# A two-layer decoder on one core: feed-forward network in parts at both ends of its run, attention bank cleared by another engine

## The reference

```python
# layer 0
x = ln(x + attn(x))                       # one head of 128
x = ln(x + xattn(x, ctx_512))             # 16 heads of 8: over own tokens (causal) and over 1601 context tokens
x = ln(x + moe(x))                        # 8 experts, 2 of them per token
# layer 1
x = ln(x + recurrent(x))                  # complex linear recurrence over the tokens
x = ln(x + S((x Wq)(ctx Wk)^T) (ctx Wv))  # one head of 128, over the 1601 context tokens
g = silu(x W1 * s1) * (x W2 * s2)         # 128 -> 512, weights of -1, 0, 1 with a scale for each column
h = gelu(gelu(g H1 * sh1) H2 * sh2)       # 512 -> 512 -> 512
x = ln(x + h W3 * s3)                     # 512 -> 128
```

## Time and profile before

| | |
|---|---|
| median of 3 runs | 692.98 us (692.75 to 695.24) |
| profiled execution, its own time | 695.09 us |
| its span, first to last instruction | 692.1 us |
| PE busy | 610.8 us (88% of the span) |
| DVE busy | 526.6 us (76%) |
| ACT busy | 449.9 us (65%) |
| POOL busy | 205.5 us (30%) |
| mean granted clock of PE | 0.974 of 2.4 GHz |

### The profile page before, as it was taken

How to read it: one execution, slowest core, us unless ns; L and a number is a source line. 1 busy time by engine, 2 the same in 40 slices (tenths; PEclk the granted TensorE clock), 3 DMA queues, 4 the chain that set the end, 5 groups by cost and what they waited for, 6 DMA issues and landing times. The chain is left out here.

```text
span 692.1 us, 13555 instructions
## 1 busy us (share of the span) xinstructions
PE 610.8 (88%) x5182; PEld 332.9 (48%) x5183; DVE 526.6 (76%) x706; ACT 449.9 (65%) x813; POOL 205.5 (30%) x277
## 2 busy tenths in 40 slices
PE   8989899999999999999999874999819899888996
PEld 5645433333333333433333353788304566547883
DVE  5369889999999999999964463899589668767442
ACT  3556578888888888888887451556782256655324
POOL 7224532335455576676640030000000000014000
PEclk9999989999999999999999997999978999999999
DMA  8258575655666544333310069553000100000000
GB/s 206 98 152 278 167 214 182 145 121 140 163 165 159 141 112 98 92 82 89 91 37 2 6 227 408 162 159 111 1 0 0 43 4 0 2 1 0 1 0 30
DMA packets 43293, 70.74 MB, mean 102 GB/s; under 512 B 12492, under 2 KB 31652, under 8 KB 42720
## 3 DMA queue, kind: packets, MB, share of 16 engines
q1 hardware_dynamic: 31696, 38.34, 20.9%
q0 software_dynamic: 10928, 29.32, 13.1%
q10 hardware_dynamic: 608, 2.25, 1.4%
HBM read 44.41 MB, written 24.79 MB: 100 GB/s over the span
## 5 line engine op out<-in xcount | busy, mean ns | idle before, releaser
L962 ACT ACTIVATE prob<-ps 128x512 f32<-128x512 f32 (+2 forms) x480 | 253.1, 582 | 46.2 <-PE ps L738 39.1
L1083 DVE TENSOR_REDUCE pm<-ps 128x2 f32<-128x1024 f32 x192 | 226.0, 1216 | 6.6 <-PE ps L700 4.8
L761 PE MATMUL ps<-prob,vst 128*9 128x256 f32 (+1 forms) x1664 | 130.1, 385 | 10.1 <-ACT o_all L950 10.1
L738 PE MATMUL ps<-qq,kc 50*128 50x256 bf16 (+1 forms) x832 | 134.1, 275 | 0.1
L700 PE MATMUL ps<-kc,qq 48*128 48x512 bf16 x384 | 116.1, 387 | 3.2 <-DVE pm L1083 2.9
L738 PEld LDWEIGHTS ps<-qq,kc 50*128 50x128 bf16 (+1 forms) x832 | 52.2, 96 | 94.2 <-ACT prob L962 69.7
L761 PEld LDWEIGHTS ps<-prob,vst 128*9 128x9 f32 (+1 forms) x1664 | 25.1, 88 | 51.7 <-ACT prob L962 39.1
L1090 DVE TENSOR_REDUCE nm<-ps 128x4 f32<-128x512 f32 (+1 forms) x32 | 30.7, 958 | 14.9 <-PE ps L688 14.9
L1677 POOL DMA_DIRECT2D w_w<-in_w x2 | 1.1, 534 | 137.2 <-PE ps L1716 137.2
L700 PEld LDWEIGHTS ps<-kc,qq 48*128 48x128 bf16 x384 | 32.9, 93 | 13.3 <-DVE pm L1083 9.4
L688 PE MATMUL ps<-masks_b 64*128 64x256 bf16 x256 | 37.6, 269 | 0.0
(11 more groups left out here) (365 smaller groups left out, 1267.2 us busy)
## 6 DMA issues: line engine op xcount, KB each, us to landing
kc<-kc_scr SPq DMA_DIRECT2D x32, 300.2 KB, 4.9
comb_bc<-comb_scr SPq DMA_DIRECT2D x7, 512.0 KB, 4.8
below<-rden_scr POOLq DMA_DIRECT2D x13, 256.0 KB, 6.8
ctx<-ctx_scr POOLq DMA_DIRECT2D x1, 3204.0 KB, 17.0
raw<-in_wexp POOLq DMA_DIRECT2D x8, 384.0 KB, 3.5
exp_scr<-raw_high POOLq DMA_DIRECT2D x8, 384.0 KB, 3.9
exp_scr<-raw_low POOLq DMA_DIRECT2D x8, 384.0 KB, 4.9
kc_scr<-hi SPq DMA_DIRECT2D x6, 400.2 KB, 4.8
```

The lines of the kernel that those rows point to most:

```text
L738: last = pe.matmul(bank[0:p, j * TQ:(j + 1) * TQ], kc[s][rows, j, t * 128:t * 128 + p], qq[s][rows, 0, j, :], start=(j == 0), stop=True, s ...
L761: last = pe.matmul(o_ps[32 * hh:32 * hh + VW, kind * TQ + q0:(kind + 1) * TQ], value[:, hh * VW:(hh + 1) * VW], prob[0:k, (NST * n + t) % ...
L962: act.activation(prob[0:p, g % P_RING, 2 * e:2 * e + 2, q0:TQ], s2[0:p, k % S2_RING, 0:2 * w].rearrange("p (i q) -> p i q", i=2), ACT.Exp, ...
L1083: dve.tensor_reduce(pm[:, m % 2, c, :, jt], banks, AX.X, ALU.max).then_inc(s1_read, 1)
```

## The change

Three edits go together.

*Start of the first cross attention.* The DVE memset of `o_ps` is gone; ACT clears the bank by a copy of `X` times 0.0 behind its last copy of values. In steps 0 and 1, where there are no value products, PE issues two products of constants (128 x 512, bf16) each into the bank of the score ring that the next step overwrites. In step 1 it first waits for the two Exps of step 0.

*Front of the FFN.* ln5 of chunk 0 moves from the fourth group into the third (means at p = 4, variance at p = 5; the Ln and Exp follow at p = 0 of the fourth, DVE at p = 1), in other banks; the last weight parts move with it. DVE takes tile 0 (`gated(0)`) before the reciprocal of the fourth group. up(2) and up(3) get banks of their own and run without waiting for the attention's end; then 24 products of the first hidden layer (tiles 0 and 1) run feature by feature before up(4) to up(7). The first hidden layer gets four banks.

*End of the FFN.* The last layer of chunk 0 runs after six of the eight tiles of the second hidden layer, its residual and ln6 start among the last two tiles. Chunk 1 is taken in two parts of 256 columns from the last layer to the store.

```diff
-                    def keep_clock(count):
+                    def keep_clock(count, bank=0):
...
                         if g >= 2:
                             outputs((g - 2) // NST, (g - 2) % NST)
+                        else:
+                            if g:
+                                pe.wait_ge(exp_done, 2 * g)
+                            keep_clock(2, 2 * (g + 1) % S2_RING)
...
+                        if h == max(late_values):
+                            act.wait_ge(v_sb, DVE_VALUES)
+                            act.wait_ge(v_act, len(values_order) - DVE_VALUES)
+                            act.activation(o_ps, X[:, 0:CH], ACT.Copy, scale=0.0).then_inc(o_zero, 1)
...
-                            if m * HALVES + i == max(late_values) + 1:
-                                dve.wait_ge(v_act, len(values_order) - DVE_VALUES)
-                                dve.memset(o_ps, 0.0).then_inc(o_zero, 1)
...
-        HIGH_AT = {(1, 0): (0,), (1, 2): (1,), (1, 4): (2,), (2, 0): (3,), (2, 2): (4,), (3, 0): (5,), (3, 1): (6,)}
-        LOW_AT = {(1, 1): (0,), (1, 3): (1,), (1, 5): (2,), (2, 1): (3,), (2, 3): (4,), (3, 1): (5,), (3, 2): (6,)}
+        HIGH_AT = {(1, 0): (0,), (1, 2): (1,), (1, 4): (2,), (2, 0): (3,), (2, 2): (4,), (2, 4): (5,), (3, 2): (6,)}
+        LOW_AT = {(1, 1): (0,), (1, 3): (1,), (1, 5): (2,), (2, 1): (3,), (2, 3): (4,), (2, 5): (5,), (3, 3): (6,)}
...
-        UP, H1, H2, Y = ((0, 2), (4, 5), (6, 7)), (1, 3), (6, 7), (0, 2)
+        UP = ((0, 2), (4, 5), (1, 3), (0, 2), (1, 3), (6, 7), (0, 2), (1, 3))
+        UP_FREED = (None, None, None, 1, 3, None, 4, 5)
+        H1, H2 = (4, 5, 0, 2), (6, 7)
+        ends = [slice(0, CH), slice(CH, CH + CH // 2), slice(CH + CH // 2, 2 * CH)]
...
-                        if b == NB - 1 and p == 0:
+                        if b == NB - 2 and p == 4:
                             pe.wait_ge(s1_red, 2 * NB)
                             pe_ln5(0)
-                        if b == NB - 1 and p == 2:
+                        if b == NB - 2 and p == PAIRS - 2:
                             pe_ln5_v(0)
...
+                up(1)
+                up(2)
+                pe_ln5(1)
+                up(3)
+                pe_ln5_v(1)
+                pe.wait_ge(full_done, 2)
+                for i in range(NM):
+                    pe.wait_ge(ha_done, i + 1)
+                    for k in range(2):
+                        done = hidden_part("h1w", ha, H1[k], k, i)
+                        if i == NM - 1:
+                            done.then_inc(h1_ps, 1)
+                for k in range(NM, len(tiles)):
                     up(k)
-                    if k == 1:
-                        pe_ln5(1)
-                    if k == 2:
-                        pe_ln5_v(1)
...
+                for k in range(2, len(tiles)):
+                    first_hidden(k)
                 pe.wait_ge(split, split_by["h2w"])
-                hidden("h2w", hb, hb_done, H2, g2_done, h2_ps)
...
+                for k in range(6):
+                    second_hidden(k)
+                last_layer(0)
+                second_hidden(6)
                 pe_ln(0)
+                second_hidden(7)
+                pe_ln2(0)
+                last_layer(1)
+                last_layer(2)
                 pe_ln(1)
-                pe_ln2(0)
+                pe_ln(2)
                 pe_ln2(1)
+                pe_ln2(2)
```

More of the change, by code:

```diff
@@ L1660, in emit_rest @@
         pe_ln, pe_ln2, act_ln, _, dve_ln, x_ready, act_log, act_exp = ln_parts(
-            st, "ln6", ps[:, 4:6, :], ps[:, 6:8, :], r7_ready, apart=True, buffers=ln_buffers)
+            st, "ln6", LN6_C, LN6_V, r7_ready, apart=True, buffers=ln_buffers, spans=ends)
         tiles = [(c, m) for c in range(NCH) for m in range(NM)]
@@ L1667, in _ @@
             def _(sp):
-                for c in range(NCH):
+                for c, end in enumerate(ends):
                     sp.wait_ge(x_ready, c + 1)
-                    sp.dma_start(out[:, c * CH:(c + 1) * CH], X[:, c * CH:(c + 1) * CH]).then_inc(stored, 16)
-                sp.wait_ge(stored, 16 * NCH)
+                    sp.dma_start(out[:, end], X[:, end]).then_inc(stored, 16)
+                sp.wait_ge(stored, 16 * len(ends))
             @block.gpsimd
@@ L1890, in _, with hidden_part @@
-                hidden("h1w", ha, ha_done, H1, g1_done, h1_ps)
-                pe.wait_ge(split, split_by["h2w"])
-                hidden("h2w", hb, hb_done, H2, g2_done, h2_ps)
-                for c in range(NCH):
-                    pe.wait_ge(hc_done, NM * (c + 1))
-                    for i in range(NM):
-                        done = passes(ps[:, Y[c], :], (high_w["w3"][:, i, :], low_w["w3"][:, i, :]), 0,
-                                      [part[:, i, :] for part in hc[c]], i == 0, i == NM - 1)
-                    done.then_inc(y_ps, 1)
+                def hidden_part(name, src, bank, k, i):
+                    c, m = tiles[k]
+                    return passes(ps[:, bank, :], (high_w[name][:, i, :], low_w[name][:, i, :]), m,
+                                  [part[:, i, :] for part in src[c]], i == 0, i == NM - 1)
@@ new lines, in last_layer @@
+                def last_layer(n):
+                    end = ends[n]
+                    c = end.start // CH
+                    at = slice(end.start - c * CH, end.stop - c * CH)
+                    for i in range(NM):
+                        pe.wait_ge(hc_done, NM * c + i + 1)
+                        done = passes(Y[n], (high_w["w3"][:, i, :], low_w["w3"][:, i, :]), 0,
+                                      [part[:, i, at] for part in hc[c]], i == 0, i == NM - 1)
+                    done.then_inc(y_ps, 1)
```

120 lines of the change are left out of this document (72 added, 48 removed).

## The result

| | before | after |
|---|---|---|
| median | 694.11 us of 4 runs (692.75 to 695.89) | **684.24 us** of 4 runs (683.23 to 685.16) |
| profiled execution, its own time | 695.09 us | 683.23 us |
| its span | 692.1 us | 681.4 us |
| PE, DVE, ACT, POOL busy | 610.8, 526.6, 449.9, 205.5 us | 607.7, 526.3, 450.6, 205.7 us |
| mean granted clock of PE | 0.974 | 0.979 |

The ratio is 0.9856, 95% interval 0.9823 to 0.9889: 1.4% faster, and clear of no change. Forecast were 685.3 us and a range of 682.5 to 688.7. The engines do nearly the same work in both; what went are mostly waits and half-clock time of PE.

What follows compares the result with a forecast made beforehand. PE, busy 88% of the span, was taken as the bound, so shortening its list or gaps shortens the kernel. The terms -2.4 - 2.7 - 3.85 + 1.26 = -7.7 us took 692.98 to 685.3 us, range 682.5 to 688.7.

Steps and rivals of the forecast that it cites:

- A: Start of the first cross attention: 0.50 us of memset and 1.92 us of clock go, 2.4 us gained.
- Rival 1: Start of the first cross attention gains only the memset, 0.5 us; time 687.2 us; chance 0.17.
- B: Second cross attention, ln5 of chunk 0 a group earlier: fourth group 3.87 us shorter, third 1.17 late, 2.7 us gained.
- Rival 2: Second cross attention: the fourth group doesn't get shorter, as ACT waits for the sums; time 688.0 us; chance 0.08.
- C: Front of the FFN: PE's gaps and slow products shrink or go, a new wait of 0.26 us comes; 3.85 us gained.
- D: End of the FFN: chunk 1 as 24 narrow products for 12 wide ones costs 1.26 us.
- 0.1675 each: End of the FFN: price in us of a 256-column product with its weight load, 4.02 us for 24.
- Moving chunk 0 forward takes nothing off its list: End of the FFN: PE is gapless through the last layer, and chunk 0's products, means and variances stay.
- Nothing: End of the FFN: halving shortens last Ln and multiply by about 0.25 us each, extra hand-overs add about 0.4 together.
- narrow products at 0.115 us: End of the FFN: a sign that the prediction is wrong, if 256-column products pass at this time.
- rival 3: End of the FFN costs nothing, 24 narrow products taking 2.76 us; time 684.0 us; chance 0.08.
- Rival 4: Front of the FFN: waits for POOL's low parts drop the clock; 72 slow products give 698.7 us; chance 0.05.

Runs made afterwards that it cites:

- e2: The kernel before with the clear of the output bank moved from DVE to ACT, without constant products: 693.05 us, ratio 0.9983.
- e3: The kernel before with the four constant products added on PE and the memset left on DVE: 693.71 us, ratio 0.9979.
- e4: The kernel before with only ln5 of chunk 0 moved a group earlier: 692.47 us, ratio 0.996.
- e13: The changed kernel with one table set for the last norm and gated tile 0 put back behind the fourth group's residual: 684.05 us, ratio 0.9845.
- e12: The changed kernel with the end of the FFN as before the change, chunk 1 in one part: 685.41 us, ratio 0.9884.
- e6: The changed kernel with chunk 1 as one part of 512 columns at the end: 687.92 us, ratio 0.9919.
- e9: The changed kernel with the variance product of chunk 0 moved out of PE's stream, behind the last mean product but one: 687.39 us, ratio 0.9901.

## Why the prediction was right

The time was 684.24 us for 685.3 forecast, 1.1 us less. By steps, against the profile of before:

- **A, forecast 2.4, measured 2.96.** The mechanism holds in both halves (e2, e3). The memset is 0.61, not 0.50, and the clock the rest, as long as the constants are there; the shares shift with the order (e2). Its size depends on the course of the clock that the profile happened to show: against e4 it is 2.43, which the forecast met. My way of pricing it, by DVE's pace of a later unit at full clock, compared like with like and came within 0.6 of the 2.96. Rival 1 (only the memset) is out.
- **B, forecast 2.7, measured 2.81** (e4 alone 2.82). The fourth group is 3.82 us shorter for 3.87, the third pays 1.01 for 1.17. Rival 2 is out: ACT never waited for the sums.
- **C, forecast 3.85, measured 4.10.** The mean product came 6.34 us after up(0), as reckoned (618.64 - 612.30). The gap before it fell by 0.83 us, not 0.46, since up(2) ends later than my 12 x 0.230: the first product of up(1) has a bare load (0.42 us to the next), and the last one's row ends 0.40 us after its start, and only from there does the trace count the gap. The 1.98 us went, the slow products went (1.6 for 1.67), the new wait is 0.32 for 0.26. What I hadn't seen is that 1.6 us of this are not there in every execution, and that the tile put forward (gated 0) costs 0.35 us at the end instead of helping (e13).
- **D, forecast +1.26, measured +0.67, by other steps than mine.** This is the term that failed. "0.1675 each" was read from four products in the chain of waits; there the first weight load of the four starts only when the products before it are through, and is bare (0.19 us), so the four are 0.19 + 4 x 0.12. The load's row is below; the split is argued from it, not tested. In the stream narrow products follow each other at 0.119: 24 take 2.86 us, +0.10. Here the formula of the Trainium skill that the prediction set against the row (109 ns) was nearer than the row. "Moving chunk 0 forward takes nothing off its list" was wrong as well, since it adds: two norm products inside the stream, 0.86 us each (0.46 of their own, 0.40 of loads behind them that nothing covers), and 0.20 us at the last tile, whose cover (the last layer of chunk 0) had been moved ahead of it. That is 1.92 us, beside the 1.77 that e12 and e6 leave for the order. By e9 the second of the two norm products costs nothing by itself, since PE would wait there anyway. "Nothing" for the halves was wrong by 1.1 us (e6). These are errors of both signs, and that they met within 0.6 us of the forecast is luck. The prediction had named narrow products at 0.115 us as a sign of being wrong; they pass at 0.119, and on this step it was wrong: rival 3 had nearly the right price for the products and a wrong total.
- Rival 4 (slow early products) is out: the clock read 1.00 from 608 to 636 us and the early products are 0.23 apart.

PE's weight loads for the earlier trace rows, in the kernel before:

```profile
592.35 0.53 PEld L1774 LDWEIGHTS ps<-qk,ctx 128*128 128x128 f32 x4 [0.39 <-issue]
```

In sum 9.2 us went for the 7.7 forecast. Of the 1.5 us between them 0.56 lie in A, 0.11 in B, 0.25 in C and 0.59 in D. From the median that the forecast started at, 692.98 us, this leads to 683.8; the rest is within what either median moves by itself. So the waits of A, B and C were understood, and D was not. That the total came so close owes something to chance: 1.6 us of C and 0.5 of A hang on a course of the clock that not every execution shows.

## What to carry to other kernels

Read a price for an operation from a stretch where it runs as it will run, and look at what stands before it: a product carries part of a weight load that the others hide when it stands behind a wait (in e9 0.22 us to the next for 0.12, at 670.75 us) or behind a product of the norm (0.40 us more). What an order seems to lose by a gap may be the cover of something else, so ask of each moved block what it had hidden: the last layer of chunk 0 hid the last Gelu, and the variance product stood in a hole. And where an effect of the clock is worth as much as the edit, cut several traces at the same hand-over points before you believe the size in one: in two traces of the changed kernel the numbered stretches agreed within 0.13 us, where its two medians lay 1.8 apart.

## What the runs showed that I had not expected

- PE's clock fell to 1.2 GHz in a stretch in which no gap was longer than 0.52 us and PE was busy for 2.60 of 4 us (e2), and stayed whole with 3.19 of 4 us and gaps of 0.41 and 0.31 us (e3). Behind one and the same gap of 1.97 us it fell in three traces and not in two. The Trainium skill, page "TensorE: Matmul & The Clock Gate", Part 1, says of the rise to full clock at a kernel's start that its moment varies between runs of one kernel. No run here was read for that rise; the falls in these traces vary too.
- The time of one kernel varies by more than any one part of the change brings: the kernel before lay between 691.30 and 698.48 us in all its runs, those with the mean clock at 0.964 at 697.1 to 698.5 and those at 0.974 at 691.3 to 694.6. Between the stages the clock read as low as 0.50 over 400 to 408 us in e3 and 1.00 there in the changed kernel.
- Taking a table load out of the last chain, with Exp and multiply of chunk 0 moved ahead, was worth 2.71 us for the load's 1.28: it had stood between work of all parts and not only of the last.
